# Convolution pipeline: two-part chunks in a ring of four, lane-wise ramps, products contiguous in PSUM

## The reference

```python
x = x + conv(group_norm(x))        # deformable convolution
t = tokens(x)
t = t + attn(layer_norm(t))        # slice attention, 8 heads of 32
t = t + ffn(layer_norm(t))         # mixture of 8 experts, top 2, hidden 512
```

```python
v = (x @ v_w + v_b).reshape(b, h, w, 8, 32)
deform = (x @ qd_w + qd_b + prior) * sigmoid(x @ qs_w + dscale) * 6.0
weights = x @ qw_w + qw_b
px, py = column + deform[..., 0], row + deform[..., 1]
samp = bilinear(v, py, px)                 # 0 outside the image
out = einsum('bhwgkc,bhwgk->bhwgc', samp, weights)
return out.reshape(b, h, w, 256) @ out_w + out_b
```

## Time and profile before

| | us |
|---|---|
| median of 3 runs | 1585.73 |
| lowest, highest | 1584.38, 1593.72 |
| the profiled execution's own time | 1589.51 |
| its span, first to last instruction | 1587.5 |
| mean granted TensorE clock, share of full | 0.811 |

### The profile page before, as it was taken

How to read it: one execution, slowest core, us unless ns; L and a number is a source line. 1 busy time by engine, 2 the same in 40 slices (tenths; PEclk the granted TensorE clock), 3 DMA queues, 4 the chain that set the end, 5 groups by cost and what they waited for, 6 DMA issues and landing times.

```text
span 1587.5 us, 50101 instructions
## 1 busy us (share of the span) xinstructions
PE 1103.0 (69%) x22444; PEld 874.2 (55%) x22444; DVE 979.3 (62%) x1555; ACT 842.2 (53%) x1059; POOL 738.0 (46%) x448
## 2 busy tenths in 40 slices
PE   3575757666787688875876788756776788575191
PEld 2454545555476577643565677533665677235191
...
DMA packets 150519, 111.06 MB, mean 70 GB/s; under 512 B 44009, under 2 KB 131874, under 8 KB 149794
## 3 DMA queue, kind: packets, MB, share of 16 engines
...
## 4 chain that ended last, share of the span: by engine, by line
PE 43%; DVE 28%; ACT 12%; issue 10%; POOL 4%; SPq 1%; DMA 1%; another core or an unknown queue 1%; POOLq 0%; DVEq 0%; ACTq 0%
PE ps L808 14%; DVE asb L1490 6%; ACT xsb L1177 5%; PE ps L793 5%; PE ps L1037 4%; PE ps L816 4%; DVE xsb L1471 4%; PE ps L1050 3%; ACT region L1252 3%; POOL picked L653 2%; DVE yr L1482 2%; DVE region L1715 2%; DVE x_tok L1499 2%; PE ps L764 1%; DVE x_tok L1731 1%
## 5 line engine op out<-in xcount | busy, mean ns | idle before, releaser
L684 POOL TENSOR_TENSOR ysb<-yr,rw 128x960 f32<-128x960 f32 (+1 forms) x180 | 384.4, 2157 | 524.9 <-PE ps L793 519.5
L1177 ACT ACTIVATE xsb<-xsb,pick 128x896 f32<-128x896 f32 (+1 forms) x288 | 434.7, 1565 | 2.1
L1490 DVE COPY asb<-ps 128x960 f32<-128x960 f32 (+1 forms) x288 | 317.6, 1107 | 98.0 <-PE ps L793 76.8
L793 PE MATMUL ps<-xsb,ysb 64*64 64x96 f32 x11008 | 333.0, 273 | 40.0 <-ACT xsb L1177 22.0
L793 PEld LDWEIGHTS ps<-xsb,ysb 64*64 64x64 f32 x11008 | 283.7, 152 | 100.0 <-issue 48.2
L808 PE MATMUL ps<-asb,vd 32*32 32x258 f32 x8192 | 232.0, 462 | 81.6 <-DVE asb L1490 61.8
L1171 ACT ACTIVATE xsb<-xsb 128x896 f32<-128x896 f32 (+1 forms) x96 | 147.8, 1540 | 226.4 <-DVE xsb L1471 225.9
L808 PEld LDWEIGHTS ps<-asb,vd 32*32 32x32 f32 x8192 | 154.6, 114 | 151.9 <-issue 124.5
L1499 DVE TENSOR_TENSOR x_tok<-x_tok,ps 128x1024 f32<-128x1024 f32 x32 | 39.1, 1221 | 240.6 <-PE ps L816 216.2
L671 POOL TENSOR_TENSOR yr<-rw,count 128x896 f32<-128x896 f32 (+1 forms) x90 | 179.7, 1997 | 14.7 <-DMA rw<-set_rows 7.3
L1471 DVE TENSOR_TENSOR xsb<-rw,count 128x896 f32<-128x896 f32 (+1 forms) x90 | 179.2, 1991 | 0.0
...
## 6 DMA issues: line engine op xcount, KB each, us to landing
...
vd<-group_values SPq DMA_DIRECT2D x128, 128.0 KB, 2.6
...
region<-sorted_rows SPq DMA_DIRECT2D x8, 512.0 KB, 6.2
expert_rows<-region SPq DMA_DIRECT2D x8, 512.0 KB, 4.4
```

What stands on the lines that cost most here:

```text
L684: pl.tensor_tensor(ysb[:, ch % 2, 0:sets, u, :], yr[:, ch % 2, 0:sets, :], rows_of(ig)[:, 2 + u, first:first + sets].rearrange("p (s o) -> ...
L793: last = pe.matmul(o[:, :, NV * q:NV * q + NV], ysb[rows, ch % 2, col, :, :].rearrange("p u y -> p (u y)"), xsb[rows, ch % 2, col, :, :], ...
L1177: act.activation(xsb[:, ch % 2, 0:sets, :, v], xsb[:, ch % 2, 0:sets, :, NV - 1], ACT.Relu, bias=pick[:, v:v + 1], scale=-1.0).then_inc(s. ...
L1490: dve.tensor_copy(asb[:, :, :, first:first + m].rearrange("p x i m -> p i x m"), ps[:, bank:bank + 2, 0:GRID * m].rearrange("p i (x m) -> ...
```

## The change

Chunks have 18, 18, 18, 16 and 16 sets with two parts each, so ten parts per group and 80 slots per image. The buffers `xsb` and `ysb` become rings of four (`DEPTH`), `yr` goes: distances in y are written, clamped and weighed in `ysb` itself, in the place of its second row. VectorE's and GpSimd's distances are issued three chunks ahead, clamping, weighing, edges and ramps two chunks ahead. `xsb` is now [set][lane 3][grid 32]. A product is written as 96 contiguous elements of PSUM, and the copy into `asb` reads PSUM with a step of 32 elements and writes runs of 12 or 15 as before. Banks go 4, 0, 2 through nine parts, and the tenth has bank 0. At a group's first part TensorE's order is side work, products, `project(ig-2)`, `contract(ig-1)`. ScalarE does two ramp instructions behind the side work of every part. Turning moves to slots 40 to 42, tiles to 43 to 66, picking to 67 to 74, addition to 75 to 79, preparation to 22 slots apart.

```diff
 SET_TILES = NI * NA
-CHUNK_SETS = (30, 28, 28)
+CHUNK_SETS = (18, 18, 18, 16, 16)
 CHUNK = max(CHUNK_SETS)
-CHUNK_FIRST = (0, 30, 58)
-PARTS = 3
-PAIRS = ((5, 5, 5), (5, 5, 4), (5, 5, 4))
+CHUNK_FIRST = (0, 18, 36, 54, 70)
+PARTS = 2
+PAIRS = ((5, 4), (5, 4), (5, 4), (4, 4), (4, 4))
+DEPTH = 4
 AM = SETS // NJ * NV
...
-PREP_SLOTS = 19
+PREP_SLOTS = 22
 COLUMN_SLOTS = tuple(range(9, 9 + COLUMN_STEPS))
...
 ROW_SLOT = 39
-TURN_ROWS_SLOTS = (41, 41, 42, 42, 43, 43)
-TILE_SLOTS = tuple(range(45, 69))
-PICK_SLOT, PICK_SLOTS = 72, 8
-ADD_SLOT = 80
-LAST_SLOT = ADD_SLOT + PICK_SLOTS
+TURN_ROWS_SLOTS = (40, 40, 41, 41, 42, 42)
+TILE_SLOTS = tuple(range(43, 67))
+PICK_SLOT, PICK_SLOTS = 67, 8
+ADD_SLOT, ADD_SLOTS = 75, 5
+LAST_SLOT = ADD_SLOT + ADD_SLOTS
 assert len(TILE_SLOTS) == ROWS + 1 and len(TURN_ROWS_SLOTS) == TURNS
...
         vd = sb("vd", [P, 2, GRID, GC])
-        yr = sb("yr", [P, 2, CHUNK, GRID])
-        ysb = sb("ysb", [P, 2, CHUNK, NU, GRID])
-        xsb = sb("xsb", [P, 2, CHUNK, GRID, NV])
+        ysb = sb("ysb", [P, DEPTH, CHUNK, NU, GRID])
+        xsb = sb("xsb", [P, DEPTH, CHUNK, NV, GRID])
         asb = sb("asb", [P, GRID, NI, AM])
...
         ps = ctx.enter_context(nc.psum_tensor("ps", [P, 8, 512], F32))
-        PRODUCT_BANK = (4, 0, 2)
+        PRODUCT_BANK = (4, 0, 2, 4, 0, 2, 4, 0, 2, 0)
         POSITIONS_MADE, EARLY_CLEAR, TURN_CLEAR, EDGE_CLEAR, ALL_MADE = 9, 10, 13, 14, 22
...
                     wait_rows(pl, ig)
-                if ch >= 2:
-                    pl.wait_ge(s.y_ready, NU * (ch - 1))
-                pl.tensor_tensor(yr[:, ch % 2, 0:sets, :],
+                if ch >= DEPTH:
+                    pl.wait_ge(s.a_summed, PARTS * (ch - DEPTH + 1))
+                pl.tensor_tensor(ysb[:, ch % DEPTH, 0:sets, NU - 1, :],
                                  rows_of(ig)[:, 1, first:first + sets].rearrange("p (s o) -> p s o", o=1)
...
                 pl.wait_ge(s.y_within, ch + 1)
-                if ch >= 2:
-                    pl.wait_ge(s.a_summed, PARTS * (ch - 1))
                 for u in range(NU):
-                    pl.tensor_tensor(ysb[:, ch % 2, 0:sets, u, :], yr[:, ch % 2, 0:sets, :],
+                    pl.tensor_tensor(ysb[:, ch % DEPTH, 0:sets, u, :], ysb[:, ch % DEPTH, 0:sets, NU - 1, :],
                                      rows_of(ig)[:, 2 + u, first:first + sets].rearrange("p (s o) -> p s o", o=1)
...
             weigh(0)
+            y_distances(2)
+            weigh(1)
             for n in range(LAST):
...
                 if part_no == 0:
+                    if ch + 3 < ALL_CHUNKS:
+                        y_distances(ch + 3)
                     if ch + 2 < ALL_CHUNKS:
-                        y_distances(ch + 2)
-                    if ch + 1 < ALL_CHUNKS:
-                        weigh(ch + 1)
+                        weigh(ch + 2)
                 side(n // SLOTS, n % SLOTS)
...
-                ch, bank = n // PARTS, PRODUCT_BANK[n % PARTS]
-                at = n % GROUP_SLOTS
+                ch, at = n // PARTS, n % GROUP_SLOTS
+                bank = PRODUCT_BANK[at]
                 pairs = PAIRS[at // PARTS][n % PARTS]
...
                             rows = slice(HALF_ROWS * i, HALF_ROWS * i + HALF_ROWS)
-                            o = ps[64 * j:64 * j + 64, bank + i, 0:GRID * NV * pairs]\
-                                .rearrange("p (x m) -> p x m", x=GRID)
-                            last = pe.matmul(o[:, :, NV * q:NV * q + NV],
-                                             ysb[rows, ch % 2, col, :, :].rearrange("p u y -> p (u y)"),
-                                             xsb[rows, ch % 2, col, :, :], start=True, stop=True,
+                            last = pe.matmul(ps[64 * j:64 * j + 64, bank + i, NV * GRID * q:NV * GRID * (q + 1)],
+                                             ysb[rows, ch % DEPTH, col, :, :].rearrange("p u y -> p (u y)"),
+                                             xsb[rows, ch % DEPTH, col, :, :].rearrange("p v x -> p (v x)"),
+                                             start=True, stop=True,
                                              skip_group_check=True)
...
                 side(b, slot)
-                if at == 0 and ig:
-                    contract(ig - 1)
-                    if ig >= 2 and (ig - 1) % G:
-                        wait_for_banks(b, slot + 1)
-                        project(ig - 2)
-                elif at == 2 and g == 0 and ig:
+                if at == 2 and g == 0 and ig:
                     wait_for_banks(b, slot + 1)
...
                     pe.wait_ge(s.y_ready, NU * (ch + 1))
-                if n >= 3:
+                if n < 3:
+                    pe.wait_ge(s.rows_copied, 2 if n == 0 else TURN_STEPS)
+                elif at == 9:
+                    pe.wait_ge(s.a_taken, n - 1)
+                else:
                     pe.wait_ge(s.a_taken, n - 2)
-                else:
-                    pe.wait_ge(s.rows_copied, 2 if n == 0 else TURN_STEPS)
                 if ig and at == 1:
...
                 products(n)
+                if at == 0 and ig:
+                    if ig >= 2 and (ig - 1) % G:
+                        wait_for_banks(b, slot + 1)
+                        project(ig - 2)
+                    contract(ig - 1)
             wait_for_banks(B - 1, SLOTS)
...
                 act.wait_ge(s.x_away, ch + 1)
-                away = xsb[:, ch % 2, 0:chunk_of(ch)[2], :, NV - 1]
+                away = xsb[:, ch % DEPTH, 0:chunk_of(ch)[2], NV - 1, :]
                 act.activation(away, away, ACT.Relu, bias=1.0, scale=-1.0).then_inc(s.x_within, 1)
...
                 sets = chunk_of(ch)[2]
-                act.activation(xsb[:, ch % 2, 0:sets, :, v], xsb[:, ch % 2, 0:sets, :, NV - 1], ACT.Relu,
+                act.activation(xsb[:, ch % DEPTH, 0:sets, v, :], xsb[:, ch % DEPTH, 0:sets, NV - 1, :], ACT.Relu,
                                bias=pick[:, v:v + 1], scale=-1.0).then_inc(s.x_ready, 1)
...
             act.wait_ge(s.small_constants, 7)
-            x_edges(0)
-            for v in range(NV):
-                x_ramp(0, v)
-            prepare(0, TURN + 2)
-            prepare(0, TURN + 3)
+            for ch in range(2):
+                x_edges(ch)
+                for v in range(NV):
+                    x_ramp(ch, v)
+                prepare(0, TURN + 2 + ch)
             for n in range(LAST):
                 ch, part_no = n // PARTS, n % PARTS
-                ahead = ch + 1 < ALL_CHUNKS
-                if ahead and part_no:
-                    x_ramp(ch + 1, 0 if part_no == 1 else 2)
                 side(n // SLOTS, n % SLOTS)
-                if ahead and part_no == 0:
-                    x_edges(ch + 1)
-                elif ahead and part_no == 1:
-                    x_ramp(ch + 1, 1)
+                if ch + 2 < ALL_CHUNKS:
+                    if part_no == 0:
+                        x_edges(ch + 2)
+                        x_ramp(ch + 2, 0)
+                    else:
+                        x_ramp(ch + 2, 1)
+                        x_ramp(ch + 2, 2)
                 if n % GROUP_SLOTS == 0 and n:
...
                     wait_rows(dve, ig)
-                if ch >= 2:
-                    dve.wait_ge(s.a_summed, PARTS * (ch - 1))
-                dve.tensor_tensor(xsb[:, ch % 2, 0:sets, :, NV - 1],
+                if ch >= DEPTH:
+                    dve.wait_ge(s.a_summed, PARTS * (ch - DEPTH + 1))
+                dve.tensor_tensor(xsb[:, ch % DEPTH, 0:sets, NV - 1, :],
                                   rows_of(ig)[:, 0, first:first + sets].rearrange("p (s o) -> p s o", o=1)
...
                 dve.wait_ge(s.y_away, ch + 1)
-                v = yr[:, ch % 2, 0:sets, :].rearrange("p s q -> p (s q)")
+                v = ysb[:, ch % DEPTH, 0:sets, NU - 1, :]
                 dve.tensor_scalar(v, v, 0.0, 1.0, ALU.max, ALU.min).then_inc(s.y_within, 1)
...
             def take(n):
-                bank = PRODUCT_BANK[n % PARTS]
+                bank = PRODUCT_BANK[n % GROUP_SLOTS]
                 first, m = first_column(n)
...
                 dve.tensor_copy(asb[:, :, :, first:first + m].rearrange("p x i m -> p i x m"),
-                                ps[:, bank:bank + 2, 0:GRID * m].rearrange("p i (x m) -> p i x m", x=GRID))\
+                                ps[:, bank:bank + 2, 0:GRID * m].rearrange("p i (m x) -> p i x m", x=GRID))\
                    .then_inc(s.a_taken, 1)
...
                         copy_rows(b, i - 1)
-                for m in share_of(slot, ADD_SLOT, PICK_SLOTS, TOP * NT):
+                for m in share_of(slot, ADD_SLOT, ADD_SLOTS, TOP * NT):
                     add_rows(b, m)
...
             y_ramp(0)
+            x_distances(1)
             y_ramp(1)
+            x_distances(2)
             sort_constants()
...
                 ig, at, ch = n // GROUP_SLOTS, n % GROUP_SLOTS, n // PARTS
-                if n % PARTS == 0 and ch + 1 < ALL_CHUNKS:
-                    x_distances(ch + 1)
```

(7 more changed lines are left out.)

## The result

The changed kernel takes 1563.5 us (median of four runs, 1556.5 to 1572.9), the kernel before 1585.5 us beside it: a ratio of 0.984, with a 95% interval of 0.981 to 0.987. That is 22 us by the medians and 25 by the ratio, where the forecast was 88. The profiled execution took 1572.9 us, the slowest of the four; its span is 1570.6, 16.9 less than before. In what follows a gain is one minus the ratio of a run, times 1585.5 us, so that kernels that ran beside different runs of the kernel before can be compared; it says "25 us" for the change.

What follows compares the result with a forecast made beforehand. No engine is full; queues waiting for each other bound the kernel, with TensorE idle 347 us. 22 + 14 + 40 + 40 + 6 + 9 - 20 - 15 - 8 = 88 us gives 1498 us; range 1430 to 1620.

Steps and rivals of the forecast that it cites:

- the slots: Turning one slot behind its 6.2 us load: TensorE may stand 5 us in three images, 15 us lost, bounds 0 to 25.
- the side chains: Shorter ScalarE pieces let gelu in sooner, 14 us; attention and image preparation behind the ramps, 40 us (0 to 80).
- The order: Group border, products and projection before contraction: 40 us of copy wait covered, 20 lost to emptying banks, 6 for addition into x.
- a part's 8 us: Ten parts per group instead of nine: one more TensorE handshake per group, 8 us lost in all, bounds 0 to 13.
- a wait above 10 us per image for sorted rows: Sign at the turning of sorted rows that would make the prediction wrong.
- Ring and lead: Ring of four, distances three chunks ahead: TensorE's 22.0 us of waiting for ramps go, bounds 15 to 25.
- The wait of products for the emptied banks: Part behind the contraction needs banks 0 and 1 emptied by ScalarE: 1.0 us per group, 20 us lost taken.
- The next link: Group's first copy into `asb` waits for the contraction's end, but its bank is needed only three parts later; nothing gained.
- The rival of the side chains: Attention's steps wait across engines whatever ramps cost, so 40 and 14 us are not won: 1552 us, chance 0.12.
- Picks: Image 2's picks move from beside the last contraction into the woven part: 9 us gained, bounds -5 to 17.
- The stepped PSUM read: VectorE's copy reads PSUM with 128 bytes between neighbours: 1151 ns for 960 taken as unchanged, upper bound 1.86 us.
- Its rival: Stepped PSUM read is slow: as slow as before at 2.1 us per copy, 1670 us at 2.4; chance 0.26.

Runs made afterwards that it cites:

- lead_one: `old_timing` with a ring of three and every producer one chunk nearer (distances two chunks ahead, ramps, clamp and weights one): 1550.6 us.
- old_timing: Changed kernel with turning, tiles, picks and additions at the kernel before's shares of an image (slots 45, 50, 80, 88): 1526.4 us, ratio 0.960.
- order_back: Changed kernel with contraction and projection put ahead of the products again at the group's border: 1573.2 us.
- timing_order_back: `old_timing` with contraction and projection ahead of the products again, as in the kernel before: 1537.0 us.
- the square: Four lane-layout kernels: ring of two with three-part chunks, or ring of four with two-part chunks; gains old/new order 52/35 and 46/63 us.
- late_stage: Changed kernel with turning, tiles, picks and additions all four slots later (44, 47, 71, 79): 1551.0 us.
- late_dense: `late_stage` with the 16 scatters and the 16 picks each in four slots instead of eight: 1546.5 us.
- middle_dense: Changed kernel with scatters four to a slot, turning from slot 43, tiles from 47, picks at 80, additions at 88: 1527.7 us.

## Why the prediction was wrong in size

The direction and the range held, and so did most durations. Of the 63 us between the forecast's 88 and the 25 measured, two terms make up nearly all, and about half each: the slots (32 us) and the side chains (34). The order's 9 us less and a part's 8 us that don't show cancel.

The step whose mechanism was wrong is the part "Slots": "TensorE may stand 5 us in each of three images: 15, bounds 0 to 25". It stood 21 us in each, 63.7 in all. Some of that was idle time it would have had anyway: putting the stage back to its old share of the image is worth 38 us by the ratios (63 against 25). That is turning, tiles, picks and additions together, and how it divides among them isn't shown. The sum had -15 + 9 = -6 for it. What the forecast got wrong was where the wait comes from. It priced the landing of a load (6.2 us) and noted that GpSimd issues the scatters chunk by chunk, but it compared slot numbers of two tables with slots of different length. In time the turning moved forward by 7% of an image, 27 us, and its last input by 5 us. It had named "a wait above 10 us per image for sorted rows" as what would make it wrong, and that is what came.

Term by term, against what the runs showed:

- **Ring and lead**, forecast 22 (15 to 25) of ramp waits: `lead_one` against `old_timing` gives 25, and the wait for ramps in the change is 2.1 us. The wait went as forecast. That the time agrees is in part luck: under the old order ring and chunks gain nothing.
- **The order**, forecast 40 - 20 + 6 = 26: 17 in `old_timing`, 11 in the change. The contraction's wait went as forecast, from 61.8 to 0.8 us. The wait of products for the emptied banks, forecast at 20, is 11.5 us. The next link, which the forecast called harmless, isn't what ate the rest. The group's first copy does wait for the contraction (153.9 us), but with the old order products wait for copies even longer: 82.8 us in `order_back` against 61.6 in the change, 44.8 in `timing_order_back` against 35.4 in `old_timing`. Of that last pair the new order takes 39.5 us from the contraction's wait (49.4 to 9.9) and 9.4 from this one. It adds 11.5 for emptied banks, 15.2 of issue before products, 6.3 for a tile's weights, and TensorE counts as busy 10.8 us longer.
- **Gelu and other side chains**, forecast 14 + 40 = 54, called the least certain: the lanes are worth 20 us on top of ring and order, the nearest that a run comes to this term. The term was mis-sized. Its 14 for gelu was too small as a wait, since all 27.6 us went; the 40, "a fifth" of TensorE's other idle time, had no row behind it, and nothing is left to show for it. The rival of the side chains was nearer here (it left the 54 out), and missed the slots as the forecast did: 1552 against 1563.5 measured, for a reason that is only half its own.
- **Picks** out of the tail, forecast 9 (-5 to 17): 3 by the ratios and not distinguishable from nothing. The last contraction won its 17 us, but the group ahead of it, from contraction to contraction, takes 41.5 us (1316.1 to 1357.6), with the picks in it; it took 33.9 before (1320.7 to 1354.6).
- **A part more per group**, forecast 8: not measured by itself. Under the old order ring and chunks together cost 6 us, within the intervals, so it isn't large.
- **The stepped PSUM read**: 1152 ns for 960. Its rival, at 0.26, is dead. The forecast's reason (the write side of PSUM is faster than VectorE) was never tested; only the duration was.
- **Durations**: ramps 776 and 718 ns where 650 and 600 were forecast, distances 0.92 us where 1.05 was, clamp 0.70 as said. The ramps' miss cost nothing visible: products wait 2.1 us for them.
- **The range**: added up, the terms' own bounds reach from about 1365 to 1613 us. The 1430 to 1550 that the forecast gives for them is narrower and doesn't hold the measured 1563.5; only the stretch towards the slow read, which never came, made the range hold it.

Adding the terms at their measured sizes in the changed structure without the slots gives 25 + 17 + 20 = 62 us, which is `old_timing`'s 63; less 38 for the slots it is the 25 us of the change. The three were each measured by taking one part away from `old_timing`. They happen to add up to its whole gain, though the square shows that they don't act independently, so the agreement is luck in part and proves nothing.

`late_stage`, which no longer waits for sorted rows, still falls 27 us short of `old_timing`. The traces show where: its picks stand 27 us for rows that aren't stored yet, chunk starts wait 46.9 us for GpSimd's weights in it and 12.2 in `old_timing`, and the last group of images 1 and 2, which has the picks, takes 50 us against 32 and 31. No run shifted `late_stage`'s picks alone; `late_dense` and `middle_dense` are the nearest pair.

What stays open: how the 38 us divide among turning, tiles, picks and additions, what the new order's issue time and busy time are, and how the gap between the forecast's 54 us for side chains and the 20 found is shared among attention, tiles and preparation.
